# Scoring one query chunk of most units during the projections, and scoring four heads at once from row quarters

## The reference

```python
q, k, v = (proj(Wq), proj(Wk), proj(Wv))           # B, 16 heads, 512, 32
scores = jnp.einsum('bhsd,bhtd->bhst', q, k) * scale
scores = jnp.where(mask[None, None, :, :], -jnp.inf, scores)
attn = jax.nn.softmax(scores, axis=-1)
out = jnp.einsum('bhst,bhtd->bhsd', attn, v)
out = out.transpose(0, 2, 1, 3).reshape(B, S, E) @ Wo.T
xn = out / rms * rms_scale * (1.0 + sc) + shift
x = x + xn
x = x + rotate(x)                                  # 4 x 128 quaternion rotation
```

## Time and profile before

| what | value |
|---|---|
| median of 3 runs | 814.6 us (812.99 to 817.53) |
| profiled execution | 813.31 us, its span 811.5 us |
| PE busy | 796.2 us, 98% |
| VectorE, ScalarE busy | 609.0 and 607.5 us, 75% each |
| GpSimd busy | 514.1 us, 63% |
| DMA | 216.62 MB, mean 267 GB/s |
| granted TensorE clock | 1.00 in every slice |

### The profile page before, as it was taken

How to read it: one execution, slowest core, us unless ns; L and a number is a source line. 1 busy time by engine, 2 the same in 40 slices (tenths; PEclk the granted TensorE clock), 3 DMA queues, 4 the chain that set the end, 5 groups by cost and what they waited for, 6 DMA issues and landing times.

```text
span 811.5 us, 16319 instructions
## 1 busy us (share of the span) xinstructions
PE 796.2 (98%) x4864; PEld 594.1 (73%) x4864; DVE 609.0 (75%) x1492; ACT 607.5 (75%) x1511; POOL 514.1 (63%) x371
## 2 busy tenths in 40 slices
PE   9999999999999899999999999999999999999987
PEld 6788888888887677677767776777677767776764
DVE  4612314213237799999999999999999999999866
ACT  6222323222326899999999999999999999999881
POOL 0899993000000011278888888888878888888894
PEclk9999999999999999999999999999999999999999
DMA  8964545546377988988999899999998999889301
GB/s 284 343 233 183 207 163 224 178 172 220 146 285 254 344 283 288 342 325 296 322 323 333 303 325 335 316 320 307 314 337 302 304 339 314 302 305 326 103 27 53
DMA packets 90575, 216.62 MB, mean 267 GB/s; under 512 B 10600, under 2 KB 11240, under 8 KB 82304
## 3 DMA queue, kind: packets, MB, share of 16 engines
q1 hardware_dynamic: 90352, 215.41, 75.8%
q10 hardware_dynamic: 144, 0.26, 0.1%
HBM read 133.81 MB, written 81.82 MB: 266 GB/s over the span
## 4 chain that ended last, share of the span: by engine, by line
PE 41%; ACT 36%; issue 9%; POOL 6%; DMA 3%; DVE 3%; SPq 1%; ACTq 0%; DVEq 0%; POOLq 0%
ACT probs L182 25%; PE banks L551 10%; PE banks L550 10%; PE banks L552 10%; ACT turned_probs L1129 7%; PE banks L889 3%; POOL late L769 3%; PE banks L924 3%; PE banks L163 3%; ACT o_T L1161 2%; DMA blocks_scratch<-staged_blocks 2%; POOL late L1267 1%; ACT inv_T L1145 1%; DMA turned_probs<-blocks_scratch 1%; PE banks L938 1%
## 5 line engine op out<-in xcount | busy, mean ns | idle before, releaser
L182 ACT ACTIVATE probs<-probs,least 128x512 f32<-128x512 f32 x512 | 393.8, 850 | 0.0
L174 DVE CUSTOM_DVE_ANT_0 probs<-banks,mask_bias 128x512 f32<-128x512 f32 x512 | 328.2, 682 | 14.5 <-PE banks L163 12.3
L889 PE MATMUL banks<-ident,probs 128*128 128x128 f32 x1568 | 230.2, 273 | 0.0
L889 PEld LDWEIGHTS banks<-ident,probs 128*128 128x128 f32 x1568 | 190.6, 140 | 42.1 <-issue 7.7
L163 PE MATMUL banks<-k_rows,q_rows 128*128 128x512 f32 x496 | 198.4, 452 | 0.2 <-issue 0.2
L1129 ACT ACTIVATE turned_probs<-banks 128x512 f32<-128x512 f32 x263 | 179.9, 712 | 8.5 <-PE banks L924 4.5
L182 ACT ACTIVATION_READ_ACCUMULATOR probs<-probs,least 128x1 f32 x512 | 168.0, 328 | 0.0
L477 DVE SCALAR_TENSOR_TENSOR late<-banks,late 128x512 fp32r<-128x512 f32 x64 | 43.9, 689 | 154.5 <-ACT late L414 154.5
L769 POOL TENSOR_TENSOR late<-rot,late 128x2048 f32<-128x2048 f32 x28 | 128.9, 4602 | 0.6 <-DVE late L1056 0.6
L414 ACT ACTIVATE late<-banks 128x512 fp32r<-128x512 f32 x64 | 38.2, 598 | 117.7 <-PE banks L552 110.6
L924 PE MATMUL banks<-turned_probs,v_sb 128*32 128x512 f32 (+1 forms) x1088 | 117.0, 570 | 6.2 <-DMA turned_probs<-blocks_scratch 4.6
(11 more groups left out here) (137 smaller groups left out, 1338.1 us busy)
## 6 DMA issues: line engine op xcount, KB each, us to landing
q_rows<-q_scratch SPq DMA_DIRECT2D x64, 512.0 KB, 6.5
k_rows<-k_scratch SPq DMA_DIRECT2D x62, 512.0 KB, 7.3
blocks_scratch<-staged_blocks SPq DMA_DIRECT2D x120, 256.0 KB, 4.6
turned_probs<-blocks_scratch SPq DMA_DIRECT2D x120, 256.0 KB, 3.5
q_scratch<-late SPq DMA_DIRECT2D x64, 256.0 KB, 2.3
k_scratch<-late SPq DMA_DIRECT2D x64, 256.0 KB, 2.3
out<-late SPq DMA_DIRECT2D x29, 256.0 KB, 4.9
raw<-in_xT SPq DMA_DIRECT2D x7, 1024.0 KB, 5.7
```

Source lines behind the costliest of these rows:

```text
L174: dve.tensor_tensor_reduce(self.probs[:, n % RING, :], self.ps[:, n % SCORE_BANKS, :], self.mask_bias[:, c, :], 1.0, 3e38, ALU.add, ALU.mi ...
L182: act.activation(self.probs[:, n % RING, :], self.probs[:, n % RING, :], ACT.Exp, bias=self.least[:, n % 32:n % 32 + 1], scale=-1.0, accum ...
L889: last = pe.transpose(turn_bank("tile", n)[:, j * P:(j + 1) * P], probs[:, n % RING, j * P:(j + 1) * P], ident[:, :])
```

## The change

- **Premade chunk.** For units 4 to 29 the four tiles of query chunk 0 (all four heads) are scored from the hi and lo parts as they lie in SBUF, masked, weighted (ScalarE) and turned in 32x32 blocks (VectorE) in the projection stage, by the new class `Made`; the unit's 1 MB goes to DRAM (`Made.store`) and comes back before its values (`load_made`, `landing`). In attention such a unit has 12 tiles instead of 16. Staging and probabilities for this are single (one unit at a time). Units 0 to 3 keep 16 tiles and turn chunk 0 in blocks as before; the half units are unchanged in work.
- **Row quarters.** `score_products` scores one query chunk of four heads: each head sits on 32 partitions, and for each of the three parts products there are four matmuls, one per row quarter and PSUM bank. Twelve matmuls with 32 rows take the place of four with 128. The four banks are one buffer: the next group of scores waits until all four masks of the group before are done.
- **Rows.** q and k, hi and lo, of a unit are one transfer of 1 MB (`row_parts`, three buffers), stored without interleaving. Tasks of q and k alternate (q0, k0, q1, k1, ...).
- **Values.** 16 products of 384 columns from PE-turned tiles and 16 of 128 columns from the landing buffer (32 matmul instructions each).
- **Order.** All tables are new; nine `probs` buffers; two turn banks instead of three. On GpSimd the rotation's products stand ahead of the split. The modulation (`mod_ready`) is made behind batch 0, and PE waits for it before batch 1. 12 early tiles instead of 13 in the last batch, where the premade chunks of units 27, 28 and 29 are made too.

```diff
-RING, SLOTS = 10, HG + 1
-EARLY = ((2, range(0, 3)), (3, range(3, 6)), (4, range(6, 8)), (5, range(8, 10)), (6, range(10, 13)))
-EARLY_BLOCKS = {4: (0, 1, 2), 5: (3,)}
-SCORE_BANKS, TURN_BANKS = 3, 3
+RING, SLOTS = 9, 3
+EARLY = ((3, (0,)), (5, (1,)), (6, (2,)))
+EARLY_BLOCKS = {5: (0, 1, 2, 3)}
+SCORE_BANKS, TURN_BANKS = HG, 2
+MADE = 4
+MADE_AT = (2, 4, 6)
...
+def score_products(pe, banks, q, k, t):
+    for way, (q_part, k_part) in enumerate(((0, 0), (0, 1), (1, 0))):
+        for i in range(HG):
+            last = pe.matmul(banks[:, i, :], q(q_part, i)[:, t], k(k_part, i), start=(way == 0), stop=(way == 2))
+    return last
...
-        if n >= SCORE_BANKS:
-            pe.wait_ge(self.masked, n - SCORE_BANKS + 1)
-        pe.matmul(self.ps[:, n % SCORE_BANKS, :], self.rows.q[:, u % 2, i, c * P:(c + 1) * P], self.rows.k_of(u)[:, i, :],
-                  start=True, stop=True).then_inc(self.scored, 1)
+        if group > 0:
+            pe.wait_ge(self.masked, HG * group)
+        score_products(pe, self.ps, lambda part, i: self.rows.head(u, part, i),
+                       lambda part, i: self.rows.head(u, 2 + part, i),
+                       slice(c * P, (c + 1) * P)).then_inc(self.scored, 1)
...
+class Made:
+    def of(self, b, m, first, last):
+        units = [NG * b + g for g, at in enumerate(MADE_AT) if m == at and not first]
+        if m == 0 and last:
+            units.append(NG * (b - 1) + NG - 1)
+        return [u for u in units if made(u)]
+    def score(self, pe, u, qk_lo_ready, early):
+        q, slot = self.rank(u), 2 * (u % 2)
+        pe.wait_ge(qk_lo_ready, 2 * NG * (u // NG) + 2 * (u % NG) + 2)
+        if q > 0:
+            pe.wait_ge(self.masked, HG * q)
+        if early > 0:
+            pe.wait_ge(self.scores.masked, HG * early)
...
+    def turn(self, dve, u):
+        q = self.rank(u)
+        if q > 0:
+            dve.wait_ge(self.stored, 16 * q)
+        for i in range(HG):
+            dve.wait_ge(self.exped, HG * q + i + 1)
+            turn_in_blocks(dve, self.staged, i, self.probs[:, i, :]).then_inc(self.turned, 1)
+    def store(self, sp, u):
+        sp.wait_ge(self.turned, HG * (self.rank(u) + 1))
+        sp.dma_start(self.scr[u], self.staged[:, :, :, :, :].rearrange("p k j i t -> p k (j i t)")).then_inc(
+            self.stored, 16)
...
                 for m in range(QKT):
                     act.wait_ge(projected, TASKS * b + tiles_of_v + m + 1)
...
+                    for u in premade.of(b, m, first, last):
+                        premade.exp(act, u)
...
+                if not last and made(NG * b - 1):
+                    premade.mask(dve, NG * b - 1)
+                    premade.turn(dve, NG * b - 1)
                 for m in range(QKT):
                     dve.wait_ge(qk_hi_ready, QKT * b + m + 1)
...
+                    if m > 0:
+                        for u in premade.of(b, m - 1, first, last):
+                            premade.turn(dve, u)
                     for n in EARLY_BLOCKS.get(m, ()) if last else ():
                         blocks.turn(dve, n)
+                    for u in premade.of(b, m, first, last):
+                        premade.mask(dve, u)
+                    for after, groups in EARLY:
+                        for group in groups if last and m == after else ():
+                            for n in range(HG * group, HG * group + HG):
+                                scores.mask(dve, n)
...
+            pe.wait_ge(mod_ready, 1)
...
+                whole = chunks == ALL
...
+                    last = pe.matmul(value_ps[i * D:(i + 1) * D, span(chunks[1:] if whole else chunks)], weights,
+                                     turned_probs[:, v % 2, 0:len(chunks) - whole, i, part, :],
                                      start=(part == 0), stop=(part == TC - 1))
+                if part == TC - 1 and whole:
+                    for j in range(TC):
+                        for i in range(HG):
...
```

482 lines of the change are left out of this document (261 added, 221 removed), and 32 rows, old and new, of tables (EXPS, MASKS, PARTS_AT, SCORES).

## The result

The changed kernel takes **880.37 us** (median of 4 runs, 879.57 to 880.61) against 814.57 for the kernel before: ratio **1.080**, 95% interval [1.077, 1.083]. Slower, by 66 us; 861 was forecast, in a range of 815 to 900. Runs over 1.5% above the fastest of the same kernel are left out of the medians here, which concerns two runs of experiment 1 alone.

What follows compares the result with a forecast made beforehand. Projection was taken as bound by PE, attention by ScalarE with PE and VectorE just behind. Profiled 813.3 + 3.5 + 49.5 + 23.4 - 28.6 = 861.1, so 861 us was forecast, range 815 to 900 (0.80).

Steps and rivals of the forecast that it cites:

- PE waits for mod_ready, +3.5: Between batches 0 and 1, PE waits for VectorE's modulation steps until 43.8 instead of going on at 40.3: +3.5 us.
- Batches 1 to 6, +49.5: Projection: premade scores and PE's waits for VectorE's lo parts bring these batches from 195.8 to 245.3 us.
- The ledger: Step-by-step projection timing of PE, VectorE, ScalarE and stores: 7.6 us loop for two passes, 41.5 us a batch.
- G: PE's cost of one row-quarter score group of four tiles, taken as 1.1 us.
- Last batch, +23.4: End of projection: 48.1 us instead of 24.8, with PE idle from about 54.7 to 63 on the batch's clock.
- Units 4 to 29, -28.6: Attention: PE takes over from ScalarE at 15.2 us a unit instead of 16.30, over 26 units: -28.6 us.
- Units 0 to 3, nil: Start of attention: 16 exps and masks kept; no cost, covered by ScalarE's 16.2 us and GpSimd's round.
- Tail, nil: Tail and half units after the whole units: they keep GpSimd's chain, so no change in time.
- Floor reached: Rival, chance 0.20: attention units at GpSimd's 14.5 us and stores landing early in projection, 830.1 us in all.
- Faster: Rival, chance 0.15: milder projection chain, VectorE's queue running ahead so PE pays little but its groups; 801.6 us in all.
- PE late in every unit: Rival, chance 0.10: attention units at 16.6 us and projection +77 us; 898 us in all.
- Quarters don't overlap: Rival, chance 0.05: row-quarter matmuls run one after another, 2.9 us a score group, units at 20.6; about 1,040 us.

Runs made afterwards that it cites:

- experiment 1: Changed kernel with nothing premade, units 4 to 29 using the order tables of units 1 to 3: 1119.7 us.
- experiment 7: Changed kernel with premade exps one task later, unit 0's block turns behind group 1's masks, and PE's mod_ready wait moved to the first premade score: 852.7 us.
- experiment 3: Changed kernel with the four exps of a premade unit one task later on ScalarE, behind the copy hi(m+1): 855.3 us.
- experiment 2: Changed kernel with nothing premade and an order table of their own for such units: 869.5 us.
- experiment 4: Changed kernel with a second staging buffer for turned scores, used by even premade units from 12 on: 871.0 us.
- experiment 8: Changed kernel with exps one task later, unit 0's block turns later, mod_ready wait moved and a second staging buffer: 841.5 us.
- experiment 5: Changed kernel with two sets of four score matmuls in every group instead of three: 856.5 us.

## Why the prediction was right, and where it was not

**Direction and mechanism held.** PE takes over from ScalarE in the units; the projection stage, already full of PE, grows by more than attention loses. 861 was 19 us too low, and each term can be set beside its measurement (spans: 878.1 - 811.5 = 66.6):

- **PE waits for mod_ready, +3.5.** PE starts batch 1 at 44.06 us instead of 40.27, 2.45 of it idle. Behind the wait seven matmuls come 0.43 us apart (clock 0.79 from 40 to 48 us), about 1.5 us more that batch 1 pays. Unit 4's group comes 3.8 us earlier when the wait is moved (experiment 7 against 3). Right.
- **Batches 1 to 6, +49.5.** Measured about +55. The ledger's batch was 41.5, the real one 42.31. G is 1.10 (6.68 us for two passes and a group in experiment 3, less 24 x 0.2325), as taken. The loop of 7.6 is 7.76. The waits are 3.7 us in batch 3 instead of 4.5. Two things the ledger did not have: in the tasks of q and k a matmul takes about 0.233 us instead of 0.2267, 0.6 us a batch, and behind two of the waits of about 2 us the clock fell, 1.6 us each time. Why those matmuls are slower is not shown; the premade work is not the reason, since with nothing premade (experiment 2) they take as long and a batch is 33.25 instead of 32.64. That G is 1.10 as taken is partly luck: the three sets and the fixed part that the prediction had add up to 0.85, and the choice of 1.1 was for the weights. Measured, the sets take 0.69 and the fixed part 0.4.
- **Last batch, +23.4.** From 295.6 to 343.06 it takes 47.5 (48.1 forecast). This nearness is partly luck. Eight passes and six groups are 28.4 us, so the ledger held some 20 us of idle PE, one wait of 8 among them. Measured are 13.8: 3.25, 6.08 and three of 1.5. The slower matmuls, and a clock of 0.84 from 300 us on, fill the rest.
- **Units 4 to 29, -28.6.** Measured -20.6. A unit is 15.35 instead of 15.2 (the terms as written add up to 15.1), which is 4 us; the other 4 are one unit, the step from values(3) to values(4), 19.04 us, where PE waits 2.0 us for a 1 MB row load at a DMA share of 1.04 and a granted clock of 0.91. The 128 columns cost 0.99 (1.2 taken), a group with both its sides about 1.14. The sum is near because errors cancel: values take 3.6 (3.9 taken), the twelve tiles' transposes 4.7 without what a group adds (4.3 taken).
- **Units 0 to 3, nil.** This step failed: "cover is ScalarE's 16.2 and GpSimd's round; without it, G - 0.91 = 0.2 a group, 3 us in 16 groups". The cover was gone, PE is full in units 1 to 3 (17.04 a unit against 16.08), and from the start of attention to values(3) it cost 5.5 us, 2.3 of them ahead of values(0). The term "four tiles cost 4 x 0.227 = 0.91" is wrong too: sixteen single scores took 4.78 us of PE in these units before, four groups take 3.62 and about 4.6 with both their sides. What grew is the transposes (5.67 a unit against 4.43) and the projection's matmuls (3.58 against 2.94).
- **Tail, nil.** 63.1 against 63.4. Right.

**What was not in the prediction.** It took the rest of the change as nearly neutral ("G - 0.91 = 0.2 a group") and put the whole loss on the premade units. Experiment 2 turns this around for the design: with nothing premade the kernel is already at 869.5, and premaking in a good order wins 28 us of that back. How much of those 56 us another table would remove stays open; units of 17.65 us still have 0.8 us of idle PE in them, and with the 17.05 of units 1 to 3 it would be an estimated 854 (26 units by 0.6 less).

**The rivals.** "Floor reached" needed units at 14.5 and stores that land early; only two sets of matmuls gave 14.66, and the store (4.8 us) stayed in the chain, as the 1.6 us a batch of experiment 4 show. "Faster" had the right view of VectorE's work: its 26.5 us a batch do fit, and once the exps stand behind hi(odd) and the staging is double PE pays little but its groups. But it counted only 1.1 us a unit there and 1.8 gained in attention; the gain is 0.95, less than G, so even experiment 8 stays above the kernel before. "PE late in every unit" needed 16.6 a unit, and "Quarters don't overlap" is out: a set of four costs 0.23. The Trainium skill (TensorE: Matmul & The Clock Gate, Measured speedup vs the span model) gives 3.07 times the rate for four quarters. This trace agrees for the whole burst: twelve matmuls of 0.227 against 0.90 us are 3.0 times, and the 1.06 worked out from the page was near the measured 1.10. By the set it is close to four times: by experiment 5 one more set costs 0.23 us, and 0.4 us of a group are fixed.

## What to carry to other kernels

Work moved from one stage to another pays only as far as its engine has slack in the stage that receives it: here a group cost PE 1.10 us in projection and the unit it left gave back 0.95, because ScalarE's relief ended at PE, 6% below. Before the work itself, look at where it stands in each engine's order: four exps ahead of one copy were worth 25 us, and a version without premade units had a ring of orders that cost 250. And price the new form of the work (bursts into all banks, new tables, fewer buffers) apart from the move that uses it: of 66 us lost, 56 are there with nothing moved.
